# A macaron block on one core: part of the prologue, of batch 0's and of batch 1's order is changed (normalisation rows first, first value products ahead of a branch, V's halves in slots 11 and 15)

## What is computed

```python
x = x + 0.5 * ffn(layernorm(x))       # ffn: fft over the features, a sparse complex 256x256 weight, ifft, real part, + bias
x = x + attention(layernorm(x))       # 16 heads of width 8, on the first 128 features; softmax(q k / 4) v, @ Wo.T + bo
x = x + 0.5 * ffn(layernorm(x))       # the same weights as the first
```

## Time and profile before

| | us |
|---|---|
| median of 3 timed runs | 313.56 |
| lowest and highest of them | 312.56, 313.92 |
| the profiled execution's own time | 312.38 |
| its span, first to last instruction | 310.5 |
| PE busy | 294.8 (95%) |
| ACT busy | 257.6 (83%) |
| DVE busy | 190.5 (61%) |
| POOL busy | 98.3 (32%) |

### The profile page before, as it was taken

The page is one execution under the profiler, slowest core; times in us unless marked ns, Lnnn a source line. Parts: engine busy times, 40 slices in busy tenths (PEclk is TensorE's granted clock), DMA queues, the critical chain, the costliest instruction groups (busy, mean ns, idle before and its releaser), DMA issues.

```text
span 310.5 us, 8810 instructions
## 1 busy us (share of the span) xinstructions
PE 294.8 (95%) x3440; PEld 112.5 (36%) x3443; DVE 190.5 (61%) x552; ACT 257.6 (83%) x285; POOL 98.3 (32%) x113
## 2 busy tenths in 40 slices
PE   8887999899998999999999999999999999998996
PEld 5633333233332333333333333334333333322333
DVE  1688546747775678657776678567755643370255
ACT  2117998898997889998998989998999999999921
POOL 6562531223604053223604251313600340034005
PEclk9999999999999999999999999999999999999999
DMA  7935615573462762665453663554372464112102
GB/s 192 337 137 192 218 65 153 195 270 133 139 217 83 245 208 103 208 204 217 155 192 129 231 205 112 198 172 143 131 238 104 138 205 170 38 68 70 37 34 70
DMA packets 25891, 49.33 MB, mean 159 GB/s; under 512 B 2032, under 2 KB 14192, under 8 KB 24048
## 3 DMA queue, kind: packets, MB, share of 16 engines
q1 hardware_dynamic: 25152, 48.26, 46.0%
q10 hardware_dynamic: 688, 0.40, 0.8%
HBM read 31.08 MB, written 17.56 MB: 157 GB/s over the span
## 4 chain that ended last, share of the span: by engine, by line
PE 75%; DMA 9%; DVE 5%; ACT 5%; issue 3%; POOL 3%; SPq 0%; ACTq 0%; POOLq 0%
PE ot L828 28%; PE misc L719 26%; PE scores L799 15%; ACT probs L669 5%; DMA leftT<-left_scr 4%; DMA q_scr<-qp 2%; PE scores L719 2%; DMA QS<-q_scr 2%; DMA left_scr<-left_blocks 1%; POOL x L553 1%; PE scores L686 1%; PE scores L693 1%; DVE left_blocks L966 1%; DVE lh L957 1%; POOL rstd L550 1%
## 5 line engine op out<-in xcount | busy, mean ns | idle before, releaser
L669 ACT ACTIVATE probs<-scores 128x1024 f32<-128x1024 f32 x256 | 243.8, 1028 | 20.6 <-PE scores L799 20.3
L828 PE MATMUL ot<-probs,VS 128*32 128x512 f32 x1024 | 133.9, 594 | 2.9 <-ACT probs L669 2.3
L799 PE MATMUL scores<-QS,KS 32*128 32x512 f32 x512 | 64.7, 495 | 3.0 <-DMA QS<-q_scr 1.3
L799 PEld LDWEIGHTS scores<-QS,KS 32*128 32x128 f32 x512 | 24.5, 181 | 109.8 <-ACT probs L669 101.0
L828 PEld LDWEIGHTS ot<-probs,VS 128*32 128x32 f32 x1024 | 30.6, 109 | 25.8 <-ACT probs L669 5.0
L563 POOL TENSOR_TENSOR x_out<-x,half_bias 128x512 f32<-128x512 f32 x7 | 9.0, 1292 | 88.8 <-DVE x L1012 88.8
L548 POOL TENSOR_SCALAR veps<-mv 128x4 f32<-128x4 f32 (+1 forms) x25 | 6.1, 242 | 95.9 <-DVE mv L946 95.9
L1017 DVE SCALAR_TENSOR_TENSOR x_out<-misc,rstd,x_out 128x256 f32<-128x256 f32 x28 | 13.5, 484 | 33.7 <-PE misc L719 30.2
L719 PE MATMUL misc<-half_ffn,xT 128*32 128x256 f32 x448 | 32.1, 386 | 0.0
L719 PE MATMUL misc<-half_ffn,xT_in 128*32 128x256 f32 x400 | 27.1, 385 | 1.4 <-DVE half_ffn L1193 1.3
L550 POOL TENSOR_TENSOR rstd<-veps,power 128x4 f32<-128x4 f32 (+1 forms) x25 | 25.3, 1013 | 2.1
(11 more groups left out here) (125 smaller groups left out, 260.0 us busy)
## 6 DMA issues: line engine op xcount, KB each, us to landing
KS<-k_scr SPq DMA_DIRECT2D x14, 512.0 KB, 4.9
QS<-q_scr SPq DMA_DIRECT2D x14, 512.0 KB, 4.6
x_in<-x SPq DMA_DIRECT2D x8, 512.0 KB, 5.1
xT_in<-x_t SPq DMA_DIRECT2D x8, 512.0 KB, 6.4
k_scr<-kp SPq DMA_DIRECT2D x8, 512.0 KB, 3.0
q_scr<-qp SPq DMA_DIRECT2D x8, 512.0 KB, 4.4
x_scr<-x_blocks SPq DMA_DIRECT2D x7, 512.0 KB, 2.9
xT<-x_scr SPq DMA_DIRECT2D x7, 512.0 KB, 4.7
```

Source lines behind the costliest of these rows:

```text
L669: nc.scalar.activation(probs[u % PRING][:, :, :], scores[u % SRING][:, :, :], ACT.Exp, scale=SCORE_SCALE).then_inc(exp_done, 1)
L799: last = mm(scores[(u + j // 2) % SRING][:, j % 2, :], KS[b % 2][rows, slot, kt * P:(kt + 1) * P].bitcast(F32R), QS[b % 2][rows, slot, :]. ...
L828: last = mm(ot[COL * j:COL * (j + 1), :], VS[b % 2][:, kt, h, :], probs[(u + j // 2) % PRING][:, j % 2, :], start=s % 8 == 0, stop=s % 8 == 7)
```

## The change

It has seven parts.

1. **Prologue, POOL and ACT.** `half_bias` is computed before ACT's third copy; POOL adds it to batch 0's first two tiles ahead of the first `rstd_of`, and the half bias of batch 1's tiles 2 and 3 is added behind the `rstd` of LN1 of batch 0. That `rstd` is made in two halves of two tiles.
2. **Prologue, DVE.** The statistics of x1 and of the next input are taken between the F1 evacuations, and `left_half(0)` is done in two halves; `F1_3` of batch 1 is evacuated behind KT and QT.
3. **First value products.** PE issues the value products of batch 0, slot 0 ahead of `guard(0)`, and again inside the exact path.
4. **SP.** `q_out(1)` is issued ahead of `k_in(1)`.
5. **Batch 0.** `N` moves to slot 10, `V_0` to slot 11, `V_1` to slot 15.
6. **Batch 1.** `F1_1`, `F1_2`, `F1_3` of batch 3 stand in slots 1, 4, 5 instead of 4, 5, 6; `left_half(3)` and `turn_left(3)` stand in slots 7 and 8 instead of 8 and 9; POOL makes LN1's `rstd` for batch 3 ahead of that of the second ffn.
7. **Batches 2 to 5.** POOL makes LN1's `rstd` ahead of `begin_x2` (two adds of 128x512), not behind.

```diff
--- before.py
+++ after.py
@@ -74,13 +74,14 @@
           12: [("F2_1a", -1, LEFT), ("F2_1", -1, LEFT)], 13: [("F2_2a", -1, LEFT), ("F2_2", -1, LEFT)],
           14: [("KT_0", 2, RIGHT)], 15: [("KT_1", 2, RIGHT)]}
 
-FIRST = {**STEADY, 0: [("F1_0a", 2, LEFT), ("F1_0", 2, LEFT)], 1: []}
+FIRST = {**STEADY, 0: [("F1_0a", 2, LEFT), ("F1_0", 2, LEFT)], 1: [("F1_1a", 2, LEFT), ("F1_1", 2, LEFT)],
+         4: [("F1_2a", 2, LEFT), ("F1_2", 2, LEFT)], 5: [("F1_3a", 2, LEFT), ("F1_3", 2, LEFT)], 6: []}
 
 BEGIN = {3: [("LT", 1, LEFT)], 4: [("KT_0", 1, RIGHT), ("F1_0a", 2, LEFT)], 5: [("F1_0", 2, LEFT), ("QT_0", 1, RIGHT)],
          6: [("KT_1", 1, RIGHT), ("F1_1a", 2, LEFT)], 7: [("F1_1", 2, LEFT), ("QT_1", 1, RIGHT)],
          8: [("F1_2a", 2, LEFT), ("F1_2", 2, LEFT)], 9: [("F1_3a", 2, LEFT), ("F1_3", 2, LEFT)],
-         10: [("V_0", 1, RIGHT), ("V_1", 1, LEFT)], 11: [("N", 1, RIGHT)], 12: [("LT", 2, LEFT)],
-         13: [("KT_0", 2, RIGHT)], 14: [("KT_1", 2, LEFT)]}
+         10: [("N", 1, RIGHT)], 11: [("V_0", 1, RIGHT)], 12: [("LT", 2, LEFT)],
+         13: [("KT_0", 2, RIGHT)], 14: [("KT_1", 2, LEFT)], 15: [("V_1", 1, RIGHT)]}
 
 LATE = {0: [("F2_3a", -2, LEFT), ("F2_3", -2, LEFT)],
         2: [("WO_0", -1, LEFT), ("WO_1", -1, RIGHT)], 3: [("WO_2", -1, LEFT), ("WO_3", -1, RIGHT)],
@@ -103,7 +104,7 @@
     if it == PROLOGUE:
 
         ahead = [(f"F1_{t}", 2) for t in range(T)]
-        jobs = [(f"F1_{t}", 1) for t in range(T)] + [("LT", 1)] + ahead + [("KT", 1), ("QT", 1), ("N", 1)]
+        jobs = [(f"F1_{t}", 1) for t in range(T)] + [("LT", 1)] + ahead[:-1] + [("KT", 1), ("QT", 1), ahead[-1], ("N", 1)]
         return {s: [(name, d, LEFT)] for s, (name, d) in enumerate(jobs)}
     if it == EPILOGUE:
 
@@ -319,6 +320,11 @@
         mv_done = [sem(f"mv_done{i}") for i in range(3)]
         veps_done = [sem(f"veps_done{i}") for i in range(3)]
         rstd_done = [sem(f"rstd_done{i}") for i in range(3)]
...
         normed = sem("normed")
         ahead_ready = sem("ahead_ready")
         left_turned = sem("left_turned")
@@ -500,8 +506,8 @@
 
             load_x(3)
             k_out(1)
+            q_out(1)
             k_in(1)
-            q_out(1)
             q_in(1)
             for it in range(1, B):
                 if it + 1 < B:
@@ -581,15 +587,20 @@
                 rstd_of(0, b + 1)
                 add_rows(x_in[b % 2], x_in[b % 2], half_bias, xb_done)
 
-            rstd_of(0, 1)
             pool.wait_ge(bias_set, 1)
             pool.wait_ge(x_loaded[0], 16)
             add_row(x1[0], x_in[0], half_bias, early_biased, slice(0, 1))
             add_row(x1[0], x_in[0], half_bias, early_biased, slice(1, 2))
+            rstd_of(0, 1)
             add_row(x1[0], x_in[0], half_bias, xb_done, slice(2, T))
             pool.wait_ge(x_loaded[1], 16)
-            add_rows(x1[1], x_in[1], half_bias, xb_done)
-            rstd_of(1, 1)
+            add_row(x1[1], x_in[1], half_bias, ahead_biased, slice(0, 2))
+            pool.wait_ge(first_mv, 1)
+            nc.gpsimd.tensor_scalar(veps[1][:, 0:2], mv[1][:, 0:2, 1], EPS, None, ALU.add).then_inc(first_veps, 1)
+            pool.wait_ge(first_veps, 1)
+            nc.gpsimd.tensor_tensor(rstd[1][0][:, 0:2], veps[1][:, 0:2], power[:, 0:2], ALU.pow).then_inc(first_rstd, 1)
+            rstd_of(1, 1, slice(2, T))
+            add_row(x1[1], x_in[1], half_bias, xb_done, slice(2, T))
             rstd_of(0, 2)
             square(kp, sq_k, kp_step, 0)
             square(qp, sq_q, qp_step, 0)
@@ -603,10 +614,12 @@
             for it in range(1, B):
 
                 end_of(it - 1)
+                if it == 1:
+                    rstd_of(1, it + 3)
                 rstd_of(2, it)
+                if it > 1 and it + 2 < B:
+                    rstd_of(1, it + 3)
                 begin_x2(it)
-                if it + 2 < B:
-                    rstd_of(1, it + 3)
                 if it + 3 < B:
                     next_x(it + 3)
             pool.wait_ge(out_stored, 32 * (B - 1))
@@ -629,12 +642,12 @@
             for piece, bank, copy in ((1, scores[0][:, 0], even[0]), (3, scores[1][:, 0], even[1])):
                 act.wait_ge(ffn_mm, piece)
                 nc.scalar.copy(copy[:, :, :], half_bank(bank)).then_inc(ffn_copied, 1)
+            act.wait_ge(bias_loaded, 16)
+            nc.scalar.mul(half_bias[:, :], bias_raw[:, :], 0.5).then_inc(bias_set, 1)
             for piece, bank, copy in ((5, scores[0][:, 0], even[2]), (6, scores[0][:, 1], odd)):
                 act.wait_ge(ffn_mm, piece)
                 nc.scalar.mul(copy[:, :, :], half_bank(bank), 0.5 / E).then_inc(ffn_copied, 1)
 
-            act.wait_ge(bias_loaded, 16)
-            nc.scalar.mul(half_bias[:, :], bias_raw[:, :], 0.5).then_inc(bias_set, 1)
             act.wait_ge(pick_loaded, 16)
             nc.scalar.copy(pick[:, :, :, :, :].rearrange("p n s i r -> p (n s i r)").bitcast(F32R),
                            pick_raw[:, :, :, :, :].rearrange("p n s i r -> p (n s i r)")).then_inc(pick_set, 1)
@@ -824,10 +837,15 @@
                 if s % 8 == 0:
                     wait(pe, ot_taken, 2 * b + g)
                 pe.wait_ge(exp_done, u + 2)
+                value_products(b, s).then_inc(quad_done, 1)
+
+            def value_products(b, s):
+                _, _, kt, heads = quad_units(s)
+                u = PAIRS * b + 2 * s
                 for j, h in enumerate(heads):
                     last = mm(ot[COL * j:COL * (j + 1), :], VS[b % 2][:, kt, h, :],
                               probs[(u + j // 2) % PRING][:, j % 2, :], start=s % 8 == 0, stop=s % 8 == 7)
-                last.then_inc(quad_done, 1)
+                return last
 
             def guard(b, taken):
 
@@ -864,6 +882,8 @@
                         pe.wait_ge(exact_taken, done + 1)
                         mm(misc[:, 0:E], attnT[:, :], wo_sb[:, :], start=True, stop=True).then_inc(exact_ready, 1)
                     pe.wait_ge(guarded, b + 1)
+                    if b == 0:
+                        value_products(0, 0)
                 with pe.Else():
                     pe.sem_inc(exact_ready, EXACT_MM)
 
@@ -901,6 +921,7 @@
             pe.wait_ge(evacuated, evac_count("N", 0))
             first_rows(3)
             score_quad(0, 1)
+            value_quad(0, 0)
             guard(0, evac_count("N", 0))
             pe.wait_ge(late_loaded, 32)
 
@@ -915,7 +936,8 @@
                     if it == 0 and 0 < s < 3:
                         keep_awake(1, misc[:, :])
                     run_jobs(it, s)
-                    value_quad(it, s)
+                    if it or s:
+                        value_quad(it, s)
                     if s == guard_slot(it) and it + 1 < B:
                         guard(it + 1, count_of_slots_to(it, s))
 
@@ -952,7 +974,8 @@
                     norm_stats(0, x_in[b % 2], t, t == T - 1)
 
             def left_half(b, tiles=range(T)):
-                dve.wait_ge(rstd_done[1], b + 1)
+                if b or tiles[-1] == T - 1:
+                    dve.wait_ge(rstd_done[1], b + 1)
                 for t in tiles:
                     last = nc.vector.tensor_scalar(lh[:, t, :], x1[b % 3][:, t, 0:HD], mv[1][:, t, 0:1],
                                                    rstd[1][0][:, t:t + 1], ALU.subtract, ALU.mult)
@@ -1202,20 +1225,41 @@
             norm0_stats(0)
             norm_moments(0, 1)
             fold(half_ffn, even[2], odd[:, :, :], ALU.subtract, ALU.add, 6, 4)
-            for s in range(T):
-                run_jobs(PROLOGUE, s)
-            norm0_stats(1)
-            left_half(0)
+            dve.wait_ge(mv_done[0], 1)
+            norm0_stats(1, range(0, 2))
+
+            def first_x1(t):
+                dve.wait_ge(evacuated, evac_count(f"F1_{t}", 0))
+                return nc.vector.bn_stats(stats[1][:, t, :], x1[0][:, t, :])
+
+            evacuate("F1_0", 0)
+            evacuate("F1_1", 0)
+            first_x1(0)
+            evacuate("F1_2", 0)
+            first_x1(1).then_inc(first_stats, 1)
+            dve.wait_ge(first_stats, 1)
+            for t in range(2):
+                last = nc.vector.bn_aggr(mv[1][:, t, :], stats[1][:, t, :])
+            last.then_inc(first_mv, 1)
+            evacuate("F1_3", 0)
+            first_x1(2)
+            first_x1(3).then_inc(stats_done[1], 1)
+            norm_moments(1, 1, range(2, T))
+            dve.wait_ge(first_rstd, 1)
+            left_half(0, range(0, 2))
+            norm0_stats(1, range(2, T))
+            left_half(0, range(2, T))
             norm_moments(0, 2)
 
-            run_jobs(PROLOGUE, T)
-            for t in range(T):
+            evacuate("LT", 0)
+            for t in range(T - 1):
                 evacuate(f"F1_{t}", 1)
-            run_jobs(PROLOGUE, 2 * T + 1)
-            run_jobs(PROLOGUE, 2 * T + 2)
+            evacuate("KT", 0)
+            evacuate("QT", 0)
+            evacuate(f"F1_{T - 1}", 1)
             dve.wait_ge(row_ready, 1)
```

(6 more changed lines are left out.)

5 lines of the change are left out of this document (added).

## The result

The changed kernel takes 314.03 us in the median of 22 runs (311.94 to 317.86), the kernel before beside it 312.46 us (22 runs, 309.68 to 315.27): a ratio of 1.0066, 95% interval 1.0042 to 1.0089. By that ratio it is 2.1 us slower, where 4 us faster was forecast. Every ratio here compares fast runs alone, those within 1.5% of the fastest of their kernel, so it is not the quotient of the medians, which lie 1.6 us apart. The profiled execution took 314.55 us, its span 312.8 us, at a granted clock of 1.0 throughout.

The account below looks back on a forecast made before the run. PE, busy for 95% of the span, was taken to bound the kernel. Gains of 1.05 + 0.4 + 0.4 + 1.1 + 1.1 = 4.05 us from a mean of 313.1 gave 309.1 us, range 307.0 to 311.5.

Parts of the forecast that it names:

- Term 1: Prologue: earlier moments let PE's transposes of the first left half start earlier; gain 1.05 us, bounds 0.4 to 1.4.
- Term 2: Batch 0's first value products: issued ahead of the guard's branch, they start earlier; gain 0.4 us, bounds 0 to 0.66.
- Term 3: Batch 0's slots 10 and 11: 3.54 us instead of 3.94 with V's halves apart; gain 0.4, bounds 0 to 0.45.
- Term 4: Batch 1's first scores: the 1.35 us stall for Q's rows goes, 0.25 charged for V_1; gain 1.1, bounds 0.9 to 1.35.
- Term 5: Left half of batch 3, made one slot earlier: PE's 1.48 us wait for it goes; gain 1.1, bounds 0 to 1.5.
- the hold as a rival: Batch 1: POOL's adds hold DVE's first two pieces of left_half(3) by 1.3 us; total 310.4 us, chance 0.06.
- Term 6: The rest, batches 2 to 5 with POOL's earlier rstd and later begin_x2: costed at nothing.
- The slower rival: Batches 2 to 5: every left half's load takes 6.05 us, losing 1.25 a batch; total 315.2 us, chance 0.04.

Follow-up runs that it names:

- q_first: The kernel before with only Q's store issued ahead of K's loads for batch 1; 0.9954 of the kernel before.
- pool_order: The kernel before with only POOL's rstd of LN1 put ahead of its adds in batches 2 to 5; 1.0011 of the kernel before.
- mended: The changed kernel with batch 0's guard in slot 14, prologue adds off DVE's fold and left half, batch 1's adds behind its left half; 0.9966 of the kernel before.
- adds_wait: The changed kernel with POOL's adds held in batches 1 to 5 until DVE has done the left half; 0.9993 of the kernel before.
- after_l: The changed kernel with SyncE's loads of the left half issued ahead of Q's rows; 1.0156 of the kernel before.
- q_first_l: q_first with SyncE's loads of the left half issued ahead of Q's rows; 1.0179 of the kernel before.
- left_whole: three_parts with all four tiles of the left half in slot 8, ahead of V's cast; 0.9936 of the kernel before.
- whole_l: left_whole with SyncE's loads of the left half issued ahead of Q's rows; 0.9924 of the kernel before.
- three_parts: mended with batch 1's left half, POOL's order and the place of the first value products as in the kernel before; 1.0010 of the kernel before.
- mended_l: mended with SyncE's loads of the left half issued ahead of Q's rows; 1.0105 of the kernel before.
- old_v: The changed kernel with batch 0's slots 10 to 15 as before, both halves of V in slot 10; 1.0018 of the kernel before.

## Why the prediction was wrong, point by point

- **Term 1 (1.05): failed, at two edits that I had costed at nothing.** I wrote "I cost the earlier `half_bias` at nothing": it lets POOL's first adds run over the fold. And "the last add of 128x512 now stands behind that power" was read as POOL being free sooner, not as an add over the last two pieces. **This is the first step that failed.** Measured: 0 in the profile of the changed kernel (the fold 0.54 longer, the last two pieces 0.95 longer), 0.5 where the bias came earlier, 0.75 with the adds apart.
- **Term 2 (0.4): nothing.** I said that behind the products the branch "shows no price". It shows 0.48 of "issue" in front of the next scores, ACT still stands 0.41 in front of its fifth exponential, and from first to third scores it is 4.2 with the edit and without.
- **Term 3 (0.4): right.** 3.54 forecast and measured. But I charged V_1 with 0.25 in slot 15 (in term 4). That holds with the guard in slot 14 (0.2 to 0.5 in seven profiles); as changed it cost 1.25. **This is the second step that failed: I had read DVE's work at that place as "work that it did anyway", and not what the evacuation of the slot before stands behind.**
- **Term 4 (1.1): right in mechanism.** The wait goes in all 14 profiles with the new order, and q_first wins 0.46%. But 1.35 was one execution's; the mean is 0.87.
- **Term 5 (1.1): the third step that failed, and its sign with it.** The term was aimed at a wait that stood in one profile at 1.48, and in six kernels with the old place of the left half was 1.48, 0, 1.38, 0.36, 0 and 0.19. Against that stands the hold, 1.4. I had the hold as a rival at 0.06, with the price right (1.3) and the place right. By the Trainium skill, GPSIMD Engine Reference, Specifications, POOL's SBUF interfaces are shared with VectorE; I held "one row only, and there it was POOL that was slow" against it. Here the trace agrees, with DVE the slow one: a piece beside an add takes 0.62 or 1.31 in batch 1, 0.34 alone. Both rows fit one reading: whichever engine started second was held (last section).
- **Term 6 (nothing): not settled.** Later left halves are held by 0.7 and nothing waits for that (pool_order). The waits for the loads behind the first one were 0.3 to 4.0 in six profiles with batch 1's left half in its old place, 2.5 in the mean, and 1.1 to 4.1, mean 3.1, in the five with it early and held. That may be 0.6 of a loss or chance: the two with it early and not held had 4.6 (mended) and 2.0 (adds_wait).
- **The sum.** Taken from the mean of Q's rows (0.87) and of the wait at KT_0 (0.57), the 2.2 lost by slot 14 would leave 0.8 us; 2.1 were measured (1.3 to 2.8). Some 1.3 are open (0.5 to 2.0 by the interval). The later loads may be a part, and so may the holds in batches 2 to 5: adds_wait, which takes these away too, gains 1.1 more than batch 1 explains, but pool_order, which has them alone, loses only 0.1% with an interval of 0.4% about it. The pair of after_l and q_first_l shows none of it.
- **The slower rival** (late left halves in every batch, 0.04) named the right resource; whether it has a share in the 2.1 us is the open part above.

## What to carry to other kernels

Before an add is moved on POOL, list what DVE does beside it: a fold of two SBUF operands and a scaling from SBUF to SBUF were held for as long as the add went on, statistics, transposes and casts out of PSUM were not, and where the next DVE instruction releases PE the hold is a stall. A wait on a DMA in one profile is a sample, not a price: look at a second execution of the same kernel before it enters a sum. Where several loads share one deadline, changing their order moves the wait; making the first of them ready earlier, in a gap in which the engine waits anyway, took most of it away here (2.5 us of such waits in left_whole and 1.6 in whole_l, 0.9936 and 0.9924 of the kernel before; 4.2 and 6.3 in three_parts and mended_l). Alone, on the kernel before, the same edit gave 0.9963, which is not clear of noise.

## What the runs showed of the hardware

The hold lasts to the end of the add, and no longer. In the 11 profiles that have them, 53 pieces of the left half start beside an add of 128x512. They take 0.60 to 1.32 us, and each ends 0.08 to 0.09 us behind the end of the add that was running when it started; no other piece took over 0.35. These adds keep 1.27 to 1.30. Statistics (0.41), casts out of PSUM (0.42) and transposes (0.72) beside such adds keep their time. Where DVE started first it was POOL that took longer: the first eps before (0.49 in place of 0.24, DVE's fold had started 0.03 earlier), and in the changed kernel the second add of 128x256 (1.00, the first took 0.72), which started 0.01 behind the first half of the fold.

A long wait of PE for a load is at times followed by a drop of its clock. pool_order, stretches of half a microsecond on PE (length, busy, granted clock, DMA share, GB/s), around the wait of 1.75 that ends at 129.65:

```profile
128.50:129.00 0.50, 0.00 (x0) 1.00 0.07 19
129.00:129.50 0.50, 0.00 (x0) 1.00 0.07 25
129.50:130.00 0.50, 0.35 (x8) 1.00 0.01 4
130.00:130.50 0.50, 0.50 (x12) 0.80 0.00 0
130.50:131.00 0.50, 0.50 (x8) 0.50 0.00 0
...
133.00:133.50 0.50, 0.50 (x12) 0.50 0.00 0
133.50:134.00 0.50, 0.50 (x12) 0.79 0.00 0
134.00:134.50 0.50, 0.50 (x8) 1.00 0.00 0
```

The clock is at its lower level, 1.2 of 2.4 GHz, from about 130.3 to 133.7, and by my estimate (half of 3.4) the wait costs some 1.7 us more than it shows. The same stands behind waits of 2.18 (old_v, at 201 us), 1.96 (three_parts, at 234 us) and 1.90 (q_first_l, at 203 us), but not behind 2.31 in mended or 2.54 in left_whole; what decides isn't shown. It is a likely reason why kernels that are equal within 0.6 us up to batch 1's last scores (mended, three_parts) lie 0.4% apart: a mean clock of 0.995 or less stands beside one of mended's 12 timed runs and four of three_parts', and without these the means are 311.4 and 311.7 us.

The end of such a load is thin: in the last microsecond of the wait above the DMA engines are busy at a share of 0.07, about one of the sixteen, while PE stands. Why one of them is late was not tried.
